# Attention 1 of a two-layer kernel: the softmax sums taken from ScalarE's exponentials and given to VectorE

## The reference, cut to what matters

```python
x = x + layernorm(attn(layernorm(x)))          # attention 1: 4 batches, 16 heads of 16
x = x + layernorm(ffn(layernorm(x)))           # attention 2 (32 heads of 128), router, 33 experts

# attention 1
q, k, v = (x @ W.T split into heads)           # (4, 16, 256, 16) each
scores = einsum('bhqd,bhkd->bhqk', q, k) * 16 ** -0.5
scores = where(causal, scores, -inf)
attn   = softmax(scores, axis=-1)              # exp(s - max) / sum(exp(s - max))
out    = einsum('bhqk,bhkd->bhqd', attn, v) ; out @ Wo.T
```

## Time and profile before

| what | value |
|---|---|
| median of three executions | 948.99 us |
| the profiled execution | 950.87 us, its span 948.8 us |
| mean granted clock of TensorE | 0.970 |
| PE busy | 867.5 us, 91% of the span |
| DVE busy | 616.5 us, 65% |
| ACT busy | 570.5 us, 60% |
| POOL busy | 455.9 us, 48% |
| reciprocals of attention 1 (L621) | 32, at 32.9 to 171.5 us |
| exponentials of attention 1 (L573) | 128 ACTIVATE and 128 ACTIVATION_READ_ACCUMULATOR, at 29.7 to 168.8 us |

### The profile page before, as it was taken

The page is one execution under the profiler, slowest core; times in us unless marked ns, Lnnn a source line. Parts: engine busy times, 40 slices in busy tenths (PEclk is TensorE's granted clock), DMA queues, the critical chain, the costliest instruction groups (busy, mean ns, idle before and its releaser), DMA issues. The chain is left out here.

```text
span 948.8 us, 18792 instructions
## 1 busy us (share of the span) xinstructions
PE 867.5 (91%) x6108; PEld 802.1 (85%) x6108; DVE 616.5 (65%) x1620; ACT 570.5 (60%) x1570; POOL 455.9 (48%) x486
## 2 busy tenths in 40 slices
PE   5799998767999999999999999978999999999994
PEld 4699897657999998999899999867888888888884
DVE  5456667647787787778777777755444544544546
ACT  6788888656766766667666667654333333433333
POOL 3743334357867766777776777720222222221221
PEclk9799999978999999999999999997999999999998
DMA  7001000131114111421111111200433333333321
GB/s 234 1 1 46 22 23 1 59 93 39 35 46 142 38 45 35 114 66 46 34 46 35 46 45 36 51 1 18 144 116 116 114 98 115 101 114 116 112 82 45
DMA packets 50246, 63.34 MB, mean 67 GB/s; under 512 B 5728, under 2 KB 36064, under 8 KB 50176
## 3 DMA queue, kind: packets, MB, share of 16 engines
q1 hardware_dynamic: 49088, 61.41, 22.2%
q10 hardware_dynamic: 1088, 1.05, 0.3%
HBM read 41.86 MB, written 1.18 MB: 45 GB/s over the span
## 5 line engine op out<-in xcount | busy, mean ns | idle before, releaser
L639 POOL TENSOR_TENSOR b_prob<-b_prob,b_rsum 128x256 f32<-128x256 f32 (+1 forms) x128 | 104.7, 839 | 108.3 <-DVE b_rsum L621 108.3
L73 PE MATMUL banks<-act_t,b_w 128*128 128x256 f32 (+1 forms) x392 | 129.3, 330 | 3.9 <-DVE b_work L1194 2.8
L74 PE MATMUL banks<-act_t,b_w 128*128 128x256 f32 (+1 forms) x392 | 127.2, 324 | 0.0
L75 PE MATMUL banks<-act_t,b_w 128*128 128x256 f32 (+1 forms) x392 | 127.0, 324 | 0.0
L1955 ACT ACTIVATE moe_hid<-banks 128x512 fp32r<-128x512 f32 x66 | 39.5, 598 | 124.1 <-DVE banks L2046 124.1
L1355 ACT ACTIVATE b_prob<-banks,b_negmax 128x128 f32<-128x128 f32 (+1 forms) x256 | 103.6, 416 | 13.3 <-DVE b_negmax L1342 12.9
L2039 DVE TENSOR_TENSOR moe_gated<-banks,moe_share 128x512 f32<-128x512 f32 x66 | 45.6, 691 | 85.0 <-PE banks L75 80.9
L1211 ACT ACTIVATE b_qt<-b_work 128x512 fp32r<-128x512 f32 x64 | 40.5, 632 | 97.5 <-POOL b_work L1206 97.5
L639 POOL TENSOR_TENSOR a_prob<-a_prob,a_rsum 128x256 f32<-128x256 f32 x64 | 52.0, 834 | 82.2 <-DVE a_rsum L621 82.2
L1206 POOL TENSOR_TENSOR b_work<-b_work 128x512 f32<-128x512 f32 x64 | 86.7, 1355 | 9.2
L1202 POOL TENSOR_TENSOR b_work<-b_work,rope_t 128x512 f32<-128x512 f32 x64 | 84.2, 1315 | 8.2 <-DMA b_work<-b_work 8.2
(11 more groups left out here) (237 smaller groups left out, 3026.0 us busy)
## 6 DMA issues: line engine op xcount, KB each, us to landing
b_work<-b_work SPq DMA_DIRECT2D x128, 128.0 KB, 2.3
moe_share<-gates SPq DMA_DIRECT2D x32, 512.0 KB, 3.6
b_w_raw<-in_b_wq SPq DMA_DIRECT2D x4, 1024.0 KB, 5.5
b_w_raw<-in_b_wo SPq DMA_DIRECT2D x4, 1024.0 KB, 9.6
a_src_t<-act_t SPq DMA_DIRECT2D x5, 512.0 KB, 2.9
moe_w_raw<-in_wg SPq DMA_DIRECT2D x16, 128.0 KB, 2.2
moe_w_raw<-in_wu SPq DMA_DIRECT2D x16, 128.0 KB, 2.3
moe_w_raw<-in_wd SPq DMA_DIRECT2D x16, 128.0 KB, 2.3
```

Source lines behind the costliest of these rows:

```text
L73: nc.tensor.matmul(out, w_lo, m_hi, start=start, stop=False, skip_group_check=skip)
L74: nc.tensor.matmul(out, w_hi, m_lo, start=False, stop=False, skip_group_check=skip)
L75: return nc.tensor.matmul(out, w_hi, m_hi, start=False, stop=stop, skip_group_check=skip)
L639: last = self.m.nc.gpsimd.tensor_tensor(rows, rows, rsum[:, :, t:t + 1].to_broadcast([PART, 2, width]), ALU.mult)
```

## The change

`act_exp` of attention 1 no longer asks for sums. VectorE computes them from `prob` in SBUF, in a new helper that `dve_normalise` calls between its wait on `exp_done` and the reciprocal: for each of the two key widths one `reduce_sum` over both heads (128 x 2 x 128 to 128 x 2, and 128 x 2 x 256 to 128 x 2), then an increment of a new semaphore `sums_ready`, on which VectorE itself waits before the reciprocal. `AttentionB` overrides the helper with nothing.

```diff
+        self.sums_ready = sem("sums_ready")
@@ act_exp
-                k = 2 * h + t
                 last = nc.scalar.activation(self.prob[:, p, h, lo:lo + width],
                                             m.s_ps[:, h, lo:lo + width], ACT.Exp,
-                                            bias=self.negmax[:, p % 2, t, h:h + 1],
-                                            accum_out=self.sums[:, p, k:k + 1])
+                                            bias=self.negmax[:, p % 2, t, h:h + 1])
             last.then_inc(self.exp_done, 1)
@@ dve_normalise
         wait(dve, self.exp_done, 2 * P + 2)
+        self.dve_sums(dve, p, P)
         nc.vector.reciprocal(self.rsum[:, p, :], self.sums[:, p, :]).then_inc(self.rsum_ready, 1)
@@ Attention
+    def dve_sums(self, dve, p, P):
+
+        sums = self.sums[:, p, :].rearrange("p (h t) -> p h t", h=2)
+        for t in range(NTT):
+            lo, width = t * PART, (t + 1) * PART
+            last = self.m.nc.vector.reduce_sum(sums[:, :, t], self.prob[:, p, :, lo:lo + width], AX)
+        last.then_inc(self.sums_ready, 1)
+        wait(dve, self.sums_ready, P + 1)
@@ AttentionB
+    def dve_sums(self, dve, p, P):
+        pass
```

## The result

The changed kernel takes 952.17 us (median of 8 executions, 951.0 to 955.79), the kernel before, measured beside it, 947.92 us (8 executions, 945.25 to 949.4). The ratio is 1.0051 with a 95% interval of 1.0038 to 1.0064: slower by about 4.3 us. The forecast was 947.9 us with a range to 950.9 and most of its weight on no change or faster, and it was wrong. The two profiled executions are only 0.7 us apart in span (949.5 against 948.8 us), so they don't show the loss in their totals, but a difference of its size stands between them by the end of attention 1.

A forecast was written before the change was run, and what follows sets the result against it. PE was taken to bound attention 1's steady iterations and VectorE its end. Start -1.4, iteration ends -1.8 and end +2.1 gave -1.1 us: 947.9 us on the median, range 946.3 to 949.8, for 8 in 10 945.2 to 950.9.

The forecast's parts named there:

- ScalarE's part: Attention 1's exponentials: without accumulator reads a pair's four get 0.36 us shorter; five iteration ends gain 1.8 us.
- Rival A: ScalarE gives more: exponentials take L849's pitch and the five stalls go entirely; -3.3 us, 945.7 us; chance 0.32.
- The price of a sum: VectorE's two sums a pair have pitches of 0.34 and 0.71 us, together 1.05 us, 33.6 us in all.
- In the steady slots this time lies in VectorE's idle time: Steady iterations of attention 1: the sums' 1.05 us a pair fits VectorE's idle time, 0.12 us of cover left.
- Rival B: VectorE replaces ScalarE as what PE waits for, at L937 and L645; +2.25 us, 951.2 us; chance 0.23.
- B's threshold of 1.17 us: Steady slot after the first unit: limit for a pair's sums, above which VectorE and not ScalarE releases L937.
- The start: Attention 1 up to about 50 us: earlier exponentials shorten PE's waits, 1.4 us of gain, between 0.7 and 2.0.
- The end: Last pairs of attention 1, VectorE without gap: entry -0.35, three pairs of sums +3.15, wait before L856 -0.7; net +2.1 us.
- my estimate of half: Entry to the end: sums beside layer norm pieces give back half the exponentials' saving, leaving L654's release some 0.35 us earlier.
- The sum: Whole kernel: start, iteration ends and end together, -1.4 - 1.8 + 2.1 = -1.1 us, 947.9 us on the median.
- Rival C: PE's longer waits in the last pairs bring a low clock; total about +0.4 us, 949.4; chance 0.45 together with the forecast.

The follow-up runs named there:

- ScalarE's part alone: Changed kernel without any sums on VectorE, a constant standing in their tile (output not normalised); against the kernel before, ratio 0.9960 (0.9944 to 0.9975).
- sums behind the reciprocal: Kernel before, with both reductions a pair added on VectorE behind the reciprocal, over a constant tile nobody reads; ratio 1.0044 (1.0024 to 1.0063).
- repeat: Changed kernel profiled once more, nothing altered: 17.43 us an iteration and 56.83 us from pair 24's scores to attention 2.
- POOL waiting: Changed kernel, with POOL waiting for VectorE's L894 in each iteration's last slot before multiplying; against the kernel before, ratio 0.9979 (0.9960 to 0.9998).
- the first profile: First profiled execution of the changed kernel: 17.43 us an iteration and 57.85 us from pair 24's scores to attention 2.
- the smaller collisions without sums: Kernel before, with POOL held in each iteration's last slot until L885 may start, no sums added; ratio 1.0003 (0.9988 to 1.0019).

## Why the prediction was wrong, by its own steps

**ScalarE's part: right.** 4 x 0.09 = 0.36 us a pair; measured 0.37 (1.21 us from the first exponential to L858 for 1.58), and with that part alone iterations of 17.06 us for a forecast of 17.05. Rival A (the pitch of L849) didn't occur.

**The price of a sum: right.** 1.04 us from the first reduction to the reciprocal (77.18 to 78.22) for 1.05. L638 ran at 0.40 to 0.41 and 0.67 to 0.68 us throughout. The Trainium skill's lower price (VectorE: DVE Perf Modes, The TRN2 errata; an estimate of 0.33 us for 256 elements) was not met: 405 ns.

**"In the steady slots this time lies in VectorE's idle time": the step that failed.** The load did fit (sums behind the reciprocal: 17.40 us). But the sentence on POOL, that it "gets the reciprocals 1.05 us later, but the transposes that need its product are PE's in the next slot", looked only at who waits for POOL's result, and not at what VectorE runs while POOL works. POOL's 1.6 us moved from before L885 (78.40 to 80.01) onto it. L885's pair became 0.93 us longer, about 0.56 of that was covered, and the 0.37 left took ScalarE's 0.36. The forecast's 5 x 0.36 = 1.8 us became 0.1 us of loss over the four measured iterations. The row was in hand: L885 at 169.72, 0.80 us beside a busy POOL. Rival B quoted it, asked by the Trainium skill only whether the sums contend, found that they don't, and dropped the support. By the same section of the Trainium skill (SBUF — State Buffer, Who interferes with whom) a VectorE instruction with two SBUF inputs contends with a GpSimd instruction that reads SBUF, and L885 is one. The runs agree on both sides: the one-input sums keep their time beside a busy POOL (679 ns in the mean, sums behind the reciprocal), and L885 is held until the POOL instruction in flight has ended. B's threshold of 1.17 us was not the point either: L946 at 91.69 follows the reciprocal at 91.44 by 0.25 us, the cover was used up as computed, and nothing came of it.

**The start: mis-sized, and only roughly measured.** Pair 8's scores are 1.4 us earlier in both profiles (60.85 for 62.21, and 60.55 for 61.99), where the start's 1.4 and the first iteration end's 0.36 were forecast. But this mark scatters by as much from one kernel to the next. In the five profiles whose exponentials accumulate it lies at 60.63 to 62.21 us, 61.63 in the mean (the 60.63 is that of the sums behind the reciprocal, which changes nothing on ScalarE); in the eight where they don't, at 59.86 to 61.40, 60.57 in the mean. That is 1.1 us for a forecast of 1.8, and ScalarE's part alone had 0.8.

**The end: mis-sized, and the largest part of the loss.** Forecast +2.1 = -0.35 + 3.15 - 0.7. Measured +4.3 (repeat) and +5.3 us. By the repeat's marks, counted from pair 24's scores: L663 starts at 25.39 for 24.36, +1.0 where -0.35 was forecast; from there to L865 15.77 us for 13.13, +2.6 for a forecast of 2.45; from L865 to attention 2 15.66 for 15.07, +0.6 for 0. The middle term was about right: three pairs of sums, the idle time before L856 taken off. The first is wrong by 1.4 us; with POOL waiting L663 stands at 24.37, so 1.0 of it goes with the collision (L894 at 131.17, 1.41 us for its pair) and its delay passed on, and the rest is my estimate of half for the layer norm pieces. The last fits L894's second collision, 1.66 us for 1.00. The first profile adds 1.0, 0.5 of it with L1735. By this sum about 2.6 us of the loss at the end are VectorE's work and 1.6 to 2.6 collisions with what they pass on. The split is argued from the marks. The runs bear it out in part: the sums with POOL's start unmoved cost 2.8 us there, the smaller collisions without sums 1.15, and POOL's wait brought the next to last L663 2.1 us forward, though the end came out only 0.5 to 1.5 us shorter.

**The sum.** Start -1.4, iterations about 0, end +4.3 to +5.3: +2.9 to +3.9 at the start of attention 2, as the profiles show (187.11 less 184.21, and 188.41 less 184.40), against a measured 4.25 between the medians. Rival C's low clock occurred at the place that it named; in the changed kernel it cost 0.2 us at most behind L865, and whether it did so in the profile with POOL's wait is open.

What stays open: why PE's clock falls at 152 to 160 us in the first profile (0.50 and 0.76) and not in the repeat (1.00), whether that is what makes L663 0.3 us later there, and how often L1735 comes behind POOL's instruction. It could account for part of the scatter of the changed kernel (951.0 to 955.8); no run shows it.

## What to carry to other kernels

When a step delays another engine's start, list what runs beside that engine's new interval, not only who waits for its result: here 1 us of sums, free by itself, moved POOL's product onto a VectorE instruction with two SBUF inputs and cost all that ScalarE had gained in the steady part. Then ask how much of the delay is covered before the bottleneck engine waits: here 0.56 us of 0.93. Put a wait on the engine with slack (POOL) so that the pair cannot overlap; one such wait turned 0.5% slower into 0.2% faster, though in the last iteration that wait may itself delay what follows. And cost a moved load stage by stage: where the receiving engine has no gap, as VectorE in the last pairs, leave the work where it was.

## What the runs showed of the hardware

A VectorE subtraction with two SBUF inputs that meets POOL's multiplication in SBUF is held until the POOL instruction that runs then has ended, and ends about 0.14 us behind it: 1.12 us for 0.28 behind one of 1.04, 0.70 behind one of 0.64. The addition L1735, four times as many elements, ends 0.55 us behind it (158.27 and 157.72). Where VectorE started first it went first: in the repeat of the changed kernel L1735 keeps its 0.73 us and POOL's second instruction takes 1.49 for 1.04. A sum with one SBUF input is not held: 675 to 682 ns for 512 elements in 31 sums beside a busy POOL. The accumulator read of an exponential shows 209 ns of busy time and costs 93: 26.8 us of busy time went, and four exponentials became 0.37 us shorter.
